# Four 16-head attentions in one kernel: another order for TensorE, and row maxima written back in one copy

## The reference

```python
def attention(x, wq, wk, wv, wo, bo):            # _L3_ffn_ref, used twice
    b, t, _ = x.shape
    q = (x @ wq).reshape(b, t, HEADS, HEAD_DIM)  # HEADS, HEAD_DIM = 16, 8
    ...
    scores = jnp.einsum('bqhd,bkhd->bhqk', q, k)
    mask = jnp.arange(t)[:, None] < jnp.arange(t)[None, :]
    scores = jnp.where(mask, -jnp.inf, scores)
    attn = jax.nn.softmax(scores / np.sqrt(HEAD_DIM), axis=-1)
    ctx = jnp.einsum('bhqk,bkhd->bqhd', attn, v).reshape(b, t, EMB)
    return ctx @ wo + bo
```

## Time and profile before

| | |
|---|---|
| median of 3 runs | 4644.17 us (4641.49 to 4651.4) |
| profiled execution | 4657.17 us, its span 4655.4 us, granted TensorE clock 0.909 |
| busy TensorE, VectorE, ScalarE, GpSimd | 4048.3, 3020.3, 2448.4, 1222.1 us |
| exponentials (L1163, 896) | 821.0 us |
| reduces (L1199, 1280) | 805.6 us |
| `max` matmuls (L1071, 1792) | 532.4 us |
| `back` matmuls (L1115, 3584) | 453.5 us |
| `front` matmuls (L1096, 1792) | 407.2 us |
| full attentions | from 141 to 547 us, and from 1321 to 1728 us |
| causal attentions | from 3564 to 3849 us, and from 4147 to 4444 us |

### The profile page before, as it was taken

One profiled execution on the slowest core, in us unless ns is written; L12 is line 12 of the kernel. 1 busy time (PEld: TensorE's weight loads), 2 busy tenths in 40 slices (PEclk: granted clock), 3 DMA queues, 4 the chain that ended last, 5 costly groups with the idle time before them and its releaser, 6 DMA issues.

```text
span 4655.4 us, 61774 instructions
## 1 busy us (share of the span) xinstructions
PE 4048.3 (87%) x22254; PEld 1923.2 (41%) x22256; DVE 3020.3 (65%) x7202; ACT 2448.4 (53%) x4189; POOL 1222.1 (26%) x1835
## 2 busy tenths in 40 slices
PE   8888879999898889999887778898987889968899
PEld 5222245656532225555553224555554224422243
DVE  4888466777578867677344995666567763377732
ACT  3488733555448774455345553444543773326742
POOL 1100023333210003333111663111113223432234
PEclk8799978999879998899888998899997999978999
DMA  1100002111010002111000000000011100000000
GB/s 52 26 16 15 14 33 69 37 33 38 8 54 22 15 35 49 33 32 36 5 7 5 0 0 9 17 9 17 9 38 25 24 14 1 30 22 22 15 0 9
DMA packets 48018, 104.14 MB, mean 22 GB/s; under 512 B 15064, under 2 KB 15064, under 8 KB 46432
## 3 DMA queue, kind: packets, MB, share of 16 engines
q1 hardware_dynamic: 46560, 98.62, 7.8%
q10 hardware_dynamic: 1152, 1.57, 0.2%
HBM read 40.37 MB, written 1.05 MB: 9 GB/s over the span
## 4 chain that ended last, share of the span: by engine, by line
PE 59%; DVE 23%; ACT 10%; POOL 3%; issue 3%; DMA 1%; ACTq 1%; SPq 0%; POOLq 0%; DVEq 0%
PE PS L448 30%; PE PS L1115 8%; PE PS L1071 6%; DVE SM L1199 6%; PE PS L2660 2%; ACT AR L455 2%; DVE AR L2464 2%; ACT AR L1163 2%; DVE AR L452 2%; PE PS L1096 2%; PE PS L1773 1%; PE PS L1763 1%; PE PS L475 1%; ACT PS L2408 1%; POOL SV L545 1%
## 5 line engine op out<-in xcount | busy, mean ns | idle before, releaser
L448 PE MATMUL PS<-AR,WS 128*128 128x512 f32 (+1 forms) x2112 | 1063.4, 643 | 77.1 <-DVE AR L452 30.8
L1163 ACT ACTIVATE AR<-PS 128x1024 f32<-128x1024 f32 (+3 forms) x896 | 821.0, 934 | 268.3 <-PE PS L1096 241.7
L1199 DVE TENSOR_REDUCE SM<-PS 128x1 f32<-128x512 f32 x1280 | 805.6, 683 | 125.2 <-PE PS L1071 122.9
L455 ACT ACTIVATE AR<-PS 128x512 f32<-128x512 f32 (+4 forms) x728 | 440.5, 615 | 507.2 <-PE PS L448 377.5
L1071 PE MATMUL PS<-AR 51*128 51x512 bf16 (+3 forms) x1792 | 532.4, 392 | 170.7 <-DVE SM L1199 105.7
L448 PEld LDWEIGHTS PS<-AR,WS 128*128 128x128 f32 (+1 forms) x2112 | 403.9, 203 | 544.0 <-issue 412.6
L1115 PE MATMUL PS<-AR 128*32 128x512 f32 (+3 forms) x3584 | 453.5, 579 | 9.1 <-POOL AR L1251 7.5
L1844 ACT ACTIVATE AR<-PS,SM 128x128 f32<-128x128 f32 x512 | 229.9, 453 | 426.3 <-DVE SM L1907 420.7
L1071 PEld LDWEIGHTS PS<-AR 51*128 51x128 bf16 x1792 | 132.2, 94 | 712.0 <-DVE SM L1199 425.4
L1096 PE MATMUL PS<-AR 51*128 51x512 bf16 (+3 forms) x1792 | 407.2, 369 | 14.4 <-ACT AR L1163 13.3
L1985 POOL TENSOR_TENSOR AR<-AR,SM 128x256 f32<-128x256 f32 x256 | 162.8, 636 | 555.7 <-DVE SM L1911 555.7
(11 more groups left out here) (322 smaller groups left out, 7226.0 us busy)
## 6 DMA issues: line engine op xcount, KB each, us to landing
TP<-RAW SPq DMA_DIRECT2D x512, 64.0 KB, 2.0
AR<-AR SPq DMA_DIRECT2D x720, 32.0 KB
WS<-wall SPq DMA_DIRECT2D x4, 3654.5 KB, 11.3
WS<-wall SPq DMA_DIRECT2D x8, 902.5 KB, 4.5
WS<-wall SPq DMA_DIRECT2D x2, 3334.5 KB, 10.9
WS<-wall SPq DMA_DIRECT2D x1, 2384.0 KB, 9.1
WS<-wall SPq DMA_DIRECT2D x1, 1543.5 KB, 6.2
AR<-AR ACTq DMA_DIRECT2D x48, 32.0 KB
```

Of the source, the lines that this page charges most:

```text
L448: t = e.matmul(o, l, r, start=(n == 0), stop=(n == len(pairs) - 1))
L455: return e.activation(o, i, ACT.Copy, scale=1.0)
L1163: e.activation(pv[:, :, off:512], sv[:, :, off:512], ACT.Exp, scale=scale).then_inc(*F.at_exp.up((s, u, p2)))
L1199: e.tensor_reduce(top, bank(ring(n + g), m), AX.X, ALU.max).then_inc(*F.at_max.up((s, k, i, rr, k0, g)))
```

## The change

The list is now made by a small calculation in time. It keeps a clock for each engine with a fixed duration for each entry, and takes next, again and again, the entry whose start plus an urgency (`URGE`, in ns, by kind) is the smallest. So `front` entries can stand together, `back` can stand alone, and `finish` can come much later. The order of the `max` entries, of the units and of the operations in an entry is as before. Beside this:

- `WHOLE` (True for both kinds): the 4 turning matmuls become 4 pairs of accumulating matmuls. The first of each copies the 115 partitions of `Q5` as they are (zeros in the three rows), the second adds the turned maxima at rows 0 to 2 and 64 to 66; ScalarE writes all 115 rows back with one copy of 115x512. Partitions 51 to 63 of `Q5`, which nothing wrote before, are filled with zeros by one more DMA per tile (3 per attention), and `pad` has 16 rows for it.
- `MBT` has four buffers in place of two, and the copied sums have four slots (`slot(2 * (k % 2) + qc)`) in place of two. `DEEP` is 2 (as before) and `HALVES` False (no split of a `back`).

The core of the diff (the branches of the calculation for `finish`, `turn` and `out`, which only move the clocks on, are left out; so are the old rule and the lines of `DEEP` and `HALVES`):

```diff
+URGE = {False: {"front": -470, "rows": -190, "max": -500, "back": 20, "finish": 20, "turn": 600, "out": 600},
+        True: {"front": 220, "rows": -50, "max": -160, "back": 410, "finish": 100, "turn": 600, "out": 600}}
+DEEP = {False: 2, True: 2}
+WHOLE = {False: True, True: True}
@@ def attention_order(causal)
+    def ready():
+        first, both = banks[taken % 3], max(banks[taken % 3], banks[(taken + 1) % 3])
+        if issued < len(pairs):
+            k, i, rr, k0 = pairs[issued]
+            last = i % 2 and rr and (issued + 1 == len(pairs) or pairs[issued + 1][0:3] != (k, i, rr))
+            if (k < 3 or k - 3 in ended) and not (last and k and (k - 1, i) not in rows):
+                yield max(both, (0, 12000, 26000)[k] if k < 3 else ended[k - 3] + 20000), "max"
+        if parts:
+            yield max(parts[0][0], first), "rows"
+        if fronts < 2 * len(units):
+            u, p2 = divmod(fronts, 2)
+            k, qc, _, _ = units[u]
+            if (k, 4 * qc + 3) in rows and (u < deep or u - deep in used):
+                yield max(score_free[p2], rows[k, 4 * qc + 3]), "front"
+        k, qc, kti, nk = units[min(backs, len(units) - 1)]
+        if backs < len(units) and (backs, 1) in exps and (kti < nk - 1 or k < 2 or (k - 2, qc) in finished):
+            late = 600 * masked(backs)
+            yield max(exps[backs, 1] + after_act + late, sums_free if kti == 0 else 0), "back"
+        for name, line in (("finish", sums), ("turn", divided), ("out", turned)):
+            if line:
+                yield max(line[0][0], first), name
+
+    while True:
+        choices = list(ready())
+        if not choices:
+            return out
+        at, kind = min(choices, key=lambda x: max(pe, x[0]) + urge[x[1]])
+        pe = max(pe, at)
+        if kind == "max":
...
+            pe += m / 2.4 + 14
+            out.append(("max", taken) + pairs[issued])
+            for g in range(2):
+                dve = max(dve, pe + after_pe) + m / 0.96 + (132 if causal and k0 + m == 128 * (i + 1) else 66)
+                banks[(taken + g) % 3] = dve + after_dve
...
+        if kind == "front":
+            u, p2 = divmod(fronts, 2)
+            become("score")
+            pe += (512 - shut(u)) / 2.4 + 14
+            act = max(act, pe + after_pe, used.get(u - deep, 0)) + (512 - shut(u)) / 0.6 + 190
@@ program
-        MBT = ctx.enter_context(nc.sbuf_tensor("MBT", [128, 1024], BF16))
+        MBT = ctx.enter_context(nc.sbuf_tensor("MBT", [128, 2048], BF16))
@@ pads_sp
+                    if g == 0:
+                        e.dma_start(Q5[z][51:64, :, :], pad[3:16, 0:2048]).then_inc(*F.pad_in.up((s, z, "gap"), 16))
@@ attention_pe, rows
-                            l = MBT[:, 512 * ((i // 2) % 2) + 256 * q2 + 128 * r2:512 * ((i // 2) % 2) + 256 * q2 + 128 * r2 + 67]
-                            t = mm(e, p[0:67, 256 * r2 + 128 * q2:256 * r2 + 128 * q2 + 128], (l, H["I"]))
+                            l = MBT[:, 512 * (i // 2) + 256 * q2 + 128 * r2:512 * (i // 2) + 256 * q2 + 128 * r2 + 115]
+                            place = slice(256 * r2 + 128 * q2, 256 * r2 + 128 * q2 + 128)
+                            if WHOLE[causal]:
+                                was = Q5[k % 3][0:115, r2, ts_(i - 1 + q2)]
+                                t = mm(e, p[0:115, place], (H["I"][0:115, 0:115], was), (l, H["I"]))
@@ attention_pe, finish
-                        t = e.transpose(bank(p)[:, ts_(i)], slot(qc)[:, ts_(i)], C("I"))
+                        t = e.transpose(bank(p)[:, ts_(i)], slot(2 * (k % 2) + qc)[:, ts_(i)], C("I"))
@@ attention_act, rows
-                    copy(e, Q5[k % 3][0:3, :, pos], p[0:3, :].rearrange("p (r t) -> p r t", r=2))
-                    copy(e, Q5[k % 3][64:67, :, pos], p[64:67, :].rearrange("p (r t) -> p r t", r=2)).then_inc(*F.at_max_rows.up((s, k, i)))
+                    if WHOLE[causal]:
+                        copy(e, Q5[k % 3][0:115, :, pos], p[0:115, :].rearrange("p (r t) -> p r t", r=2)).then_inc(*F.at_max_rows.up((s, k, i)))
@@ attention_act, back
+                        if k >= 2:
+                            w.wait_ge(*F.at_sums_turned.on((s, k - 2, qc)))
                         w.wait_ge(*F.at_pv.on((s, u)))
-                        copy(e, slot(qc), bank(7)).then_inc(*F.at_sums.up((s, k, qc)))
+                        copy(e, slot(2 * (k % 2) + qc), bank(7)).then_inc(*F.at_sums.up((s, k, qc)))
@@ attention_pool, max
-                    if pair >= 2:
-                        w.wait_ge(*F.at_max_turned.on((s,) + pairs_of_max[pair - 2]))
+                    if pair >= 4:
+                        w.wait_ge(*F.at_max_turned.on((s,) + pairs_of_max[pair - 4]))
```

More of the change, by code:

```diff
@@ L320, in attention_order @@
     pairs = [(k, i, rr, k0) for k in range(8) for i in range(8) for rr in range(2)
              for k0 in range(0, 128 * (i + 1) if causal else 1024, 512)]
-    wide = lambda p: (min(512, 128 * (p[1] + 1) - p[3]) if causal else 512) + 90
-    halves = 2 * len(units)
-    rate = sum(wide(p) for p in pairs) / halves
-    begin = {}
-    for n, (k, qc, kti, nk) in enumerate(units):
-        begin.setdefault((k, qc), 2 * n)
-    lead, total = 0, 0
-    for p in pairs:
-        total += wide(p)
-        lead = max(lead, total - rate * (begin[p[0], p[1] // 4] - 7))
@@ L332, in attention_order @@
-    out, waiting, taken = [], [], [0]
-    def put(kind, banks, *args):
-        out.append((kind, taken[0]) + args)
-        taken[0] += banks
-    def settle(now):
-        for item in sorted([x for x in waiting if x[0] <= now], key=lambda x: x[0]):
-            waiting.remove(item)
-            put(*item[1:])
-    issued, n = 0, 0
-    def maxima(until, now):
-        nonlocal issued, n
-        while n < len(pairs) and issued + wide(pairs[n]) / 2 <= until:
-            k, i, rr, k0 = pairs[n]
-            put("max", 2, *pairs[n])
-            issued += wide(pairs[n])
-            n += 1
-            if i % 2 and rr and (n == len(pairs) or pairs[n][0:3] != (k, i, rr)):
-                waiting.append((now + 4, "rows", 1, k, i))
-            if now < 0:
-                now += 1
-                settle(now)
@@ L358, in attention_order @@
-    maxima(lead, -1000)
-    rest = [x[0] for x in waiting]
-    for z, x in enumerate(list(waiting)):
-        waiting[z] = (x[0] - max(rest) + 4,) + x[1:]
-    for h in range(halves):
-        u, p2 = divmod(h, 2)
-        maxima(lead + rate * (h + 1), h)
-        put("front", 0, u, p2)
-        if p2 and u:
-            put("back", 0, u - 1)
-            k, qc, kti, nk = units[u - 1]
-            if kti == nk - 1:
-                waiting.append((h + 2, "finish", 1, k, qc))
-                if (k, qc) == (3, 1):
-                    for c in range(2):
-                        waiting.append((h + 6 + 4 * c, "turn", 1, c))
-                        waiting.append((h + 9 + 4 * c, "out", 1, c))
-        settle(h)
@@ L376, in attention_order @@
-    put("back", 0, len(units) - 1)
-    settle(halves + 100)
-    put("finish", 1, 7, 1)
-    for c in (2, 3):
-        put("turn", 1, c)
-    for c in (2, 3):
-        put("out", 1, c)
-    return out
+    wide = lambda p: min(512, 128 * (p[1] + 1) - p[3]) if causal else 512
+    shut = lambda u: max(0, 128 * units[u][2] - 512 * units[u][1]) if causal else 0
+    masked = lambda u: causal and 128 * units[u][2] >= 512 * units[u][1]
+    after_pe, after_act, after_dve = 210, 95, 140
+    pe = act = dve = pool = 0.0
@@ new lines, in attention_order, with become @@
+    shape = "score"
+    banks, taken, issued, fronts, backs, half = [0.0] * 3, 0, 0, 0, 0, 0
+    score_free, sums_free, exps, rows, used, ended, finished = [0.0, 0.0], 0.0, {}, {}, {}, {}, set()
+    parts, sums, divided, turned, out = [], [], [], [], []
+    def become(new):
+        nonlocal pe, shape
+        pe += 100 * (shape != new)
+        shape = new
+    def ready():
[19 more added lines that the diff above has]
+                yield max(line[0][0], first), name
@@ L1003, in program @@
         PR = [AR[:, 20480 + 1024 * r:21504 + 1024 * r] for r in range(3)] + [AR[:, 11264:12288]]
[L1004 removed]
+        MB = [MBT[:, 512 * r:512 * r + 512].rearrange("p (n g m) -> p n g m", n=4, g=2) for r in range(4)]
         MF = [SM[:, 64 + 64 * r:96 + 64 * r] for r in range(3)]
@@ L1101, in attention_pe @@
                 if kind == "back":
-                    u = args[0]
+                    u, t0, t1 = args
                     k, qc, kti, nk = units[u]
                     b, a = divmod(k, 4)
-                    off = max(0, 128 * kti - 512 * qc) if causal else 0
                     if u == 0 or u == len(units) // 2:
```

98 lines of the change are left out of this document (84 added, 14 removed).

## The result

The changed kernel takes 4531.27 us (median of 4 runs, 4527.08 to 4543.54), the kernel before in the same comparison 4642.83 us (4635.36 to 4651.4): a ratio of 0.9753, 95% interval 0.973 to 0.9775, or 112 us less. The forecast was 95 us less. The profiled execution has a span of 4525.2 us at a granted clock of 0.917; the one of before had 4655.4 us at 0.909. That pair of clocks turns out to be part of the answer.

The account below looks back on a forecast made before the run. TensorE and VectorE hand work to each other, VectorE fullest yet idle 209 us in the attention bodies. Full 47 plus causal 68 less 20 us gives 95 off the 4644.2 median: 4549 us, forecast range 4515 to 4600 (0.66).

Parts of the forecast that it names:

- The order: Full attentions: `back` without a `front` in most gaps between `max` entries removes three quarters of 11.6 us, -9 us each.
- Row copies: At each `rows`, one ScalarE copy for two holds the bank 0.58 us less: net -10.6 us per full attention, 10 causal.
- `finish`: Causal: VectorE's waits of 20.7 and 26.6 us fall to 0.49 us each, saving 14.4 and 20; full ones keep 0.49.
- Causal gaps: Causal bodies: gaps holding `front` and `back` fall from 83 to 33, 11 us, of which 5 taken per attention.
- The lead "gives nothing by itself": Stretch of maxima before the first `front`: shortening it gains nothing by itself, since VectorE's work is the same.
- Tail: After the last `max`, full: six fewer `front`s, -5.6 us, two `out`s added, +1.8, net -3.8; causal gains 2 us.
- New waits: Second of two adjacent `front`s waits for the last exponential's bank: 5 us lost per attention, 20 for four.
- rival 1: ScalarE paces the body; the late second `front` costs 25 us per attention, gain only 15, 4629 us; chance 0.10.
- Rival 3: Banks at `rows` and `finish` held longer than before: +22 us in each attention, 4732 us; chance 0.05.
- Rival 4: TensorE's granted clock falls to 0.75 in all bodies: +180 us against -95, 4729 us; chance 0.03.
- The sum: Whole kernel: 47 us from full attentions plus 68 from causal ones, less 20 of new waits, gives 95 us.

Follow-up runs that it names:

- paired fronts: Kernel before, full attentions alone: second `front` of each unit moved next to the first, `back` alone behind the next `max`; 4627.36 us, ratio 0.9952.
- pairs: Kernel before, causal attentions alone: the two `front`s of a unit stand together; 4637.61 us, ratio 0.9972.
- late finishes: Kernel before, causal attentions alone: `front`s of a unit together and `finish` nine half units later; 4644.92 us, ratio 0.9978.
- the long lead: Changed kernel, causal attentions alone: no `front` before all 24 maxima of the first group; 4551.06 us, ratio 0.9779 to the kernel before.
- the list granted more: Kernel before, causal attentions: `front`s together, `finish` nine half units later, each `rows` and `finish` between the two `front`s; 4617.58 us, ratio 0.9925.

## Why the prediction was right, point by point

- **The order: right in place, and too small.** Three quarters of 11.6 us, -9 for a full attention. The 0.22 us waits went as described; paired fronts alone give 6.5 and 8.0 us. In the changed kernel VectorE's waits in the full body are 22.0 us in place of 42.2 (35.4 + 6.8): 5 less at `finish`, and 15 less on `max`, of which about 12 are those outside `rows`.
- **Row copies: the step that failed.** "Per `rows` 0.58 us less holds the bank", -10.6 us a full and -10 a causal attention, 41 us of the sum. The copy's duration was right (0.60), and the eight matmuls span 0.68 us where four spanned 0.41 (forecast +0.22). But holding the bank shorter is worth nothing in the list of before (ratio 0.9996) nor in the new one (4540 us with, 4537 without it). The 0.82 us at a `rows` is a reduce missing from VectorE's queue. My own row said so, had I taken it apart: 0.82 - 0.22 is the 0.6 of one reduce. Only with paired fronts in the old list is the copy seen to hold VectorE up, by 0.37 to 0.54 us at each `rows`, and there the single copy wasn't run. What I credited to the copies came from the list. Which part of it isn't shown: moving `rows` behind `back` in the old list gives 13.5 and 14.4 us in each full attention, more than the 10.6 forecast, but the new list does something else (19 of its 29 `rows` stand ahead of a `back` and still cost 0.85 us), and reaches the same length.
- **`finish`: right wait, wrong price.** Causal 6.0 and 6.0 us were forecast near 7 and measured 6.0 and 6.0. But taking that wait out alone made the kernel 0.2% slower, 0.1% at one clock. In a stretch paced by TensorE, VectorE's waits are a share of TensorE's time and no sum to be subtracted from. In full I kept 0.49 us each (6.8 in all); it is 1.6 in all, up to 5 us more than forecast.
- **Causal gaps: mis-sized.** 5 us were taken. At a clock of 0.93, by 1.6 us for each 0.01, first to last `max` is 257 us before, 249 with pairs, 248 with late finishes too, 237 for the new list with the long lead and 233 for the new list. So some 8 us are pairs, 1 late finishes, 4 the lead, and about 11 remain for how the calculation spreads the rest, in which TensorE stands far less at the ring (34.0 us to 4.3). No single edit of the old list brought those 11, and they aren't split further.
- **The lead "gives nothing by itself": wrong in causal,** by 6 us per attention, 2 of them in the tail. In causal TensorE sets the pace, and in the lead it has only maxima to do. For full attentions, where VectorE sets it, no run tests the sentence.
- **Tail:** -5.6 us was forecast for the `front`s and +1.8 for the `out`s. Last `max` to last `front` went from 23.3 to 19.5, 3.8 less; with the `out`s it is 30.7 to 28.1, so -2.6 where -3.8 was forecast.
- **New waits, 20 us: not there.** TensorE waits for an exponential at `front` 5.3 us in the whole kernel, which refutes rival 1. Rival 3 asked for at least 1.1 us of VectorE's time at each of the 43 `rows` and `finish`; all its waits on TensorE in the full body are 22.0 us, about 0.5 each. Rival 4 reads its own price wrongly by two: a mean lower by 0.05 over 240 us is 24 us at 1.2 GHz, not 12. The price by the hundredth, and so the 180 us, is the same.
- **The sum: right because errors cancel.** Two terms weren't there: 41 us for the copies and 34 for the causal `finish`. In their place stand about 14 us more in each full attention (28), the lead (4 for each causal one, 8), late finishes (2), the spreading in causal (11, 22), some 3 more for each causal attention's pairs (6), and the 20 us of new waits that didn't come: 86 against 75. Put together, a full attention gains 24 us up to its last `max` and 3 in the tail, and a causal one at equal clock 8 + 1 + 4 + 11 and 2 in the tail, 106 us in all. Whole runs at one clock give 98, and some 7 more by the estimate on the leads. Full bodies were forecast near 320 us and are 327 and 330; causal near 205 and are 222 and 218, behind a lead that is 13 us shorter.
- **The clock: not in the sum.** Rival 4 priced only a fall. It rose a little and went with 7 to 14 us, without which some 4538 to 4545 us would have been the result. That too is luck, as the forecast of 4549 us is for a kernel at the clock of before.

## What to carry to other kernels

Where one engine runs an in-order queue and another works off a small ring, count what is queued when the first turns away for other work. A small operation that takes a bank costs one queued piece of work, and its own duration counts only where the queue behind it comes back to the ring before it has ended: look for that wait (here 0.37 to 0.54 us, in one of the lists) before pricing a shorter copy. Look also at what stands behind the next piece of ring work: with the long `back` there a `rows` cost 1.04 to 1.21 us, with short `front`s 0.35. A wait's total is only to be subtracted on the engine that sets the pace; first find out which one does in that stretch. Before an edit is credited with a fraction of a per cent, compare runs at the same granted clock.

## What the runs showed of the hardware

- The granted clock differs from run to run of the same kernel, and the time goes with it in a line that leaves 2.2 us of scatter: 3.2 us for 0.001 over 4650 us. The runs at 0.904 and those at 0.914 are 0.7% apart.
- Lists with the same matmuls are granted different clocks, 0.903 to 0.910 against 0.914 to 0.918. In the profiles the difference is in the causal bodies (0.92 and 0.87 against 0.98 and 0.95). What in the order does it isn't settled. In the list granted more, 6 of the 48 `rows` and `finish` entries stand directly ahead of a `max`, in the other 37; but that alone it can't be, since in the changed kernel they were pushed there too (37 of 48), and it kept 0.915 to 0.917. The full bodies stay at 0.96 to 0.99 in all lists, though in the list of before TensorE waits 124 times, 37.0 us, in one of them.
- A copy by ScalarE from 115 partitions of 512 columns takes 0.60 us, one from 3 partitions 0.58, one from 128 0.60: partitions are nearly free. Eight matmuls that copy and turn span 0.68 us in the timeline, the four before 0.41.
- A reduce of 128x512 that stands alone takes 0.69 us; ten without a gap take 6.26. So each time VectorE is stopped costs a little more than the wait that the profile shows.
